# A decoder layer on one core: half a key projection set between two weighting steps, a norm's scalings moved behind the spikes, one division per group of heads

## The reference, cut to what matters

```
x = x + attn(layernorm(x), ...)                 # Mamba forward and backward, then FFN
x = x + xattn(layernorm(x), ctx, ctx, mask)     # 16 heads of 16
x = x + ffn(layernorm(x), W_fc, W_proj)

def xattn(query, key, value, mask):
    q, k, v = query @ wq.T + bq, key @ wk.T + bk, value @ wv.T + bv   # split into 16 heads
    scores = where(mask == 0, -1e9, einsum('bhqd,bhkd->bhqk', q, k) / sqrt(16))
    out = einsum('bhqk,bhkd->bhqd', softmax(scores), v)               # heads side by side again
    return out @ wo.T + bo

def ffn(x, W_fc, W_proj):
    y = square(relu(x @ W_fc.T)) @ W_proj.T
    for 5 steps: mem = 0.9 * mem + y - (mem > 1);  spikes += (mem > 1)
    return spikes / 5
```

## Time and profile before

| | us | share of the span |
|---|---|---|
| runs of the kernel, median of 3 | 2731.34 | |
| profiled execution | 2730.98 | |
| its span | 2729.2 | 100% |
| PE busy (matmuls) | 2585.1 | 95% |
| DVE busy | 2283.9 | 84% |
| ACT busy | 1743.3 | 64% |
| POOL busy | 1602.4 | 59% |
| mean granted PE clock | 0.984 | |

### The profile page before, as it was taken

How to read it: one execution, slowest core, us unless ns; L and a number is a source line. 1 busy time by engine, 2 the same in 40 slices (tenths; PEclk the granted TensorE clock), 3 DMA queues, 4 the chain that set the end, 5 groups by cost and what they waited for, 6 DMA issues and landing times. The chain is left out here.

```text
span 2729.2 us, 54786 instructions
## 1 busy us (share of the span) xinstructions
PE 2585.1 (95%) x18901; PEld 1767.7 (65%) x18934; DVE 2283.9 (84%) x3333; ACT 1743.3 (64%) x2871; POOL 1602.4 (59%) x886
## 2 busy tenths in 40 slices
PE   6999999999999999999998888999999999999995
PEld 3887787787777778777787764455454545454523
DVE  5999999999999899999999949686869595959684
ACT  4878877877977888788788633635354545444342
POOL 3999999999999999999999932111111111111010
PEclk9999999999999999999999999999999999999978
DMA  3122212212221221222122042404040404040300
GB/s 124 43 74 79 82 48 79 92 36 72 89 72 52 81 82 44 71 82 80 50 77 98 17 152 87 114 11 123 2 123 2 123 2 123 2 123 2 108 2 16
DMA packets 102089, 187.07 MB, mean 69 GB/s; under 512 B 14720, under 2 KB 75264, under 8 KB 100256
## 3 DMA queue, kind: packets, MB, share of 16 engines
q1 hardware_dynamic: 101840, 183.92, 21.4%
HBM read 148.38 MB, written 35.52 MB: 67 GB/s over the span
## 5 line engine op out<-in xcount | busy, mean ns | idle before, releaser
L983 DVE TENSOR_TENSOR_SCAN h<-dA,pair 128x512 f32<-128x512 f32 x1024 | 1172.6, 1201 | 101.9 <-PE pair L476 90.6
L1122 POOL TENSOR_TENSOR hC<-h,C_rep 128x1024 f32<-128x1024 f32 x512 | 1200.8, 2370 | 72.2 <-DVE h L983 64.5
L720 ACT ACTIVATE dA<-delta,cols 128x511 f32<-128x511 f32 x1024 | 664.2, 710 | 33.8 <-DVE h L983 27.7
L476 PE MATMUL pair<-diagB,duT 64*128 64x128 f32 x8192 | 549.3, 281 | 24.9 <-DVE h L983 15.6
L476 PEld LDWEIGHTS pair<-diagB,duT 64*128 64x128 f32 x8192 | 486.4, 188 | 126.8 <-issue 96.9
L577 PE MATMUL y_bank<-ident,hC 128*128 128x128 f32 x3980 | 521.6, 277 | 12.4 <-POOL hC L1122 10.5
L577 PEld LDWEIGHTS y_bank<-ident,hC 128*128 128x128 f32 x3980 | 440.3, 141 | 105.1 <-issue 50.5
L1912 DVE CUSTOM_DVE_ANT_0 masked<-pair,mask_bias 128x512 f32<-128x512 f32 x512 | 321.8, 687 | 19.9 <-PE pair L1380 13.6
L1999 POOL TENSOR_SCALAR rstd<-mv 128x4 f32<-128x4 f32 x24 | 23.8, 992 | 453.5 <-DVE mv L1743 451.6
L1633 ACT ACTIVATE pr<-pair 128x1024 f32<-128x1024 f32 x256 | 248.4, 1022 | 50.3 <-PE pair L1380 50.2
L2028 POOL CAST m_part<-m_rest 8x512 bf16<-8x512 f32 x16 | 9.7, 604 | 415.2 <-ACT m_rest L1633 415.2
(11 more groups left out here) (185 smaller groups left out, 3240.5 us busy)
## 6 DMA issues: line engine op xcount, KB each, us to landing
C_rep<-c_rows SPq DMA_DIRECT2D x128, 512.0 KB, 4.0
qk_parts<-qk_part SPq DMA_DIRECT2D x96, 256.0 KB, 4.1
w_in<-w_in SPq DMA_DIRECT2D x16, 1024.0 KB, 4.8
k_st<-qk_parts SPq DMA_DIRECT2D x8, 1536.0 KB, 9.1
q_st<-qk_parts SPq DMA_DIRECT2D x8, 1536.0 KB, 9.4
x_in<-x SPq DMA_DIRECT2D x18, 512.0 KB, 4.1
w_out<-w_out SPq DMA_DIRECT2D x17, 512.0 KB, 4.3
mid<-x_out SPq DMA_DIRECT2D x9, 512.0 KB, 4.8
```

Of the source, the lines that this page charges most:

```text
L476: return pe.matmul(o, lhsT, rhs, start=start, stop=stop)
L720: return act.activation(o, i, fn, **kw)
L983: last = dve.tensor_tensor_scan(h[:, g % 4, i, :], dA[:, g % 4, i, :], dBu[:, i, :], 0.0, ALU.mult, ALU.add)
L1122: last = pool.tensor_tensor(hC[:, g % RING], h[:, g % 4], C_rep[:, 2 * j:2 * j + 2, :], ALU.mult)
```

## The change

Three edits, in PE's and DVE's functions of the attention pass. On PE, `project_k` can be called for a part of its sum over the input features; the first half of the next element's first key projection now stands between `weigh(7, 0)` and `weigh(7, 1)`, and the second half where the whole stood. On DVE, the four divisions of a group become one operation over all four blocks of tokens. And DVE's order behind `keep_exp(7)` becomes `normalise(2)`, `finish`, `norm_apply`, `normalise(3)`, where it was `finish`, `normalise(2)`, `normalise(3)`, and the `norm_apply` behind `keep_exp(1)` goes.

```diff
--- before.py
+++ after.py
@@ -1451,9 +1451,17 @@
                                         ident[:, :])
                 last.then_inc(G.full_sem(("mt", i)), 1)
 
-            def project_k(beta, m, it):
-                pe.wait_ge(s_ctx.sem, s_ctx.count(beta))
-                project(("k", m), lambda k: w_att[:, 1, k, m * P:(m + 1) * P], lambda k: ctxT[:, k, :], KD, it)
+            def project_k(beta, m, it, parts=range(KD)):
+
+                key = ("k", m)
+                if 0 in parts:
+                    pe.wait_ge(s_ctx.sem, s_ctx.count(beta))
+                    pe.wait_ge(*G.free(key, it))
+                bk = G.bank(key, it)
+                for k in parts:
+                    last = mm(bk[:, :], w_att[:, 1, k, m * P:(m + 1) * P], ctxT[:, k, :], k == 0, k == KD - 1)
+                if KD - 1 in parts:
+                    last.then_inc(G.full_sem(key), 1)
 
             def project_v(jj, it):
                 project_tokens(("v", jj), tok(ctxT), lambda k: w_att[:, 2, k, :], KD, jj, it)
@@ -1587,11 +1595,13 @@
                     for half in range(2):
                         if unit + 1 < H // 2:
                             score(b, unit + 1, half)
+                        elif half == 1 and more:
+                            project_k(b + 1, 0, it, (0,))
                         weigh(b, unit, half, it)
                     if unit % 2 == 0 and unit > 0:
                         to_tokens(unit // 2 - 1, it)
                 if more:
-                    project_k(b + 1, 0, it)
+                    project_k(b + 1, 0, it, (1,))
                 to_tokens(H // 4 - 1, it)
                 if more:
                     project_k(b + 1, 1, it)
@@ -1803,10 +1813,8 @@
                 dve.reciprocal(rsum[:, :, :], o[:, :, :, DH:DH + 1].squeeze(3))
                 dve.drain()
                 dst = o_sb[:, :, g * 4 * DH:(g + 1) * 4 * DH].rearrange("p j (h e) -> p j h e", h=4)
-                for j in range(TT):
-                    last = dve.tensor_tensor(dst[:, j], o[:, j, :, 0:DH],
-                                             rsum[:, j, :].unsqueeze(2).broadcast_to((P, 4, DH)), ALU.mult)
-                last.then_inc(G.done_sem(("ot", g)), 1)
+                dve.tensor_tensor(dst, o[:, :, :, 0:DH], rsum[:, :, :].unsqueeze(3).broadcast_to((P, TT, 4, DH)),
+                                  ALU.mult).then_inc(G.done_sem(("ot", g)), 1)
 
             def spikes(beta, cols_of=(A3,)):
 
@@ -1920,8 +1928,6 @@
                 keep_exp(b, 0)
                 step(1, (1, 2))
                 keep_exp(b, 1)
-                if more:
-                    norm_apply(ATT, b + 1, x1n, xn_q)
                 step(2, (0,))
                 keep_exp(b, 2)
                 step(2, (1, 2))
@@ -1938,8 +1944,10 @@
                 keep_exp(b, 6)
                 step(4, (1, 2))
                 keep_exp(b, 7)
+                normalise(2, it)
                 finish()
-                normalise(2, it)
+                if more:
+                    norm_apply(ATT, b + 1, x1n, xn_q)
                 normalise(3, it)
                 if more:
                     cut_lo(b + 1, 0)
```

## The result

The changed kernel took 2741.31 us (median of 9 runs, 2737.18 to 2744.18) against 2731.52 us for the kernel before (median of 9, 2728.81 to 2733.31): a ratio of 1.0032, 95% interval 1.0023 to 1.0040. The forecast was 2737.5, the range ended at 2740. The direction was right, the time lies 1.3 us outside. The profiled execution took 2739.3 us, its span is 2737.5 us, 8.3 more than before. So of the 3.8 us between the forecast and the median, 2.1 are in the trace (8.3 where 6.2 was forecast), and the rest is that the median lies 2.0 us above the profiled execution, where 0.36 was assumed.

The account below looks back on a forecast made before the run. The output transfer's landing, then ACT's four copies, was taken to set the start of `wo`, with PE's list 0.17 us ahead. Seven rounds at +0.92 less 0.20 gave +6.2: 2731.34 + 6.2 = 2737.5 us, range 2732 to 2740.

Parts of the forecast that it names:

- What bounds the kernel, and the order of `finish`: Behind `keep_exp(7)`: later `finish` delays the output's landing, ACT's copies and `wo` by 0.92 us in each of seven rounds.
- The half projection: PE's gap ahead of `weigh(7, 1)` takes in 0.9 us of work, which comes out again as waiting for DVE and ACT.
- The single division: DVE's normalisation: one 128x256 operation at 417 ns for four in 0.62 us, saving 0.20 us a group.
- rival 3: DVE's division saves more, up to 0.40 us a group (0.47 by the skill's rule): +4.6, 2735.9 us; chance 0.06.
- The moved scalings: DVE's 1.38 us of norm scalings taken from behind `keep_exp(1)`: worth nothing there, ACT being only 0.04 us away.
- The last round: No next element and no wait for the output; PE waits 1.04 us for `normalise(3)`, so the shorter division gives 0.20 us.
- From there the order is as it was, everything hangs on `wo`: Behind the start of `wo`: nothing has slack to take in the delay, so all 0.92 us a round stays.
- The first round: Counted as one of the seven loop rounds, each 0.92 us longer.
- The sum: Whole profiled execution: 7 x 0.92 - 0.20 = +6.2 us, 2730.98 to 2737.2 us.
- The offset of the median, and the spread of the runs: Measured time against profile: median 0.36 us above the profiled execution, spread of runs 1 us.
- The upper bound of the sum: With the division losing 0.06 us a group, 1.18 us a round: 8.3 + 0.1 = +8.4 us.
- Rival 1: The output's landing does not hold ACT, `wo` follows PE: 0.7 us gained a round, 2726.2 us; chance 0.10.

Follow-up runs that it names:

- early_finish_whole: Changed kernel with spikes pulled ahead so `finish` stands before `keep_exp(7)`, key projection whole again behind `weigh(7, 1)`: 2732.75 us, ratio 1.0009, round 133.71 us.
- half_only: Kernel before, with only half of the next key projection moved between the last two weighting steps: 2730.98 us, ratio 0.9999, round 133.51 us.
- order_only: Kernel before, with only `normalise(2)` put ahead of `finish`: 2740.07 us, ratio 1.0031, round 134.62 us.
- finish_first: Changed kernel with `finish` back ahead of `normalise(2)`, directly behind `keep_exp(7)`: 2733.55 us, ratio 1.0012, round 133.70 us.
- one_division_only: Kernel before, with only the four divisions of a group made one of 128x256: 2732.16 us, ratio 1.0006, round 133.71 us.
- padded_once: Changed kernel with 12 idle semaphore increments of DVE ahead of its first round, run once: 2737.57 us, ratio 1.0024, round 134.43 us.
- own_tmp: Changed kernel with `tmp` in its own memory, so ACT doesn't wait for the output transfer: 2727.79 us, ratio 0.9987, round 133.10 us.
- once_16: Changed kernel with 16 idle semaphore increments of DVE ahead of its first round, run once: 2739.09 us (one execution), round 134.72 us.

## Why the prediction was right in its mechanism and wrong in its size

- **What bounds the kernel, and the order of `finish`:** right in the loop's rounds, to 0.01 us. The wait for the landing decides when `wo` starts; shift 0.92 forecast, 0.92 seen; issue 0.28 behind the end of `finish`, release 3.04 behind the issue, both as carried over. PE's path was not 0.17 us ahead of the landing's but level with it (`early_finish_whole`), which changes nothing in the sum.
- **The half projection:** right. It fills the gap and is worth 0.01 us alone (`half_only`).
- **The single division:** 425 ns against the 417 estimated, mean of the four of a round; saved 0.20 a group as taken, where rival 3 has 0.40 or 0.47. Rival 3 is out.
- **The moved scalings:** right, no effect on the units.
- **The last round:** right. PE's wait ahead of its transposes is 0.85 us (1.04).
- **"From there the order is as it was, everything hangs on `wo`":** this is the step that failed first. The order of the work was as it was, but not the place of the code. I priced the single division by its duration alone and left out that it also takes 12 instructions out of every round, and so moves the code of the maxima, where DVE and PE hand over to each other every 0.6 us. Measured price: 134.63 - 134.43 = 0.20 us a round, 1.2 us in the six distances, for an edit that the sum had as a gain.
- **The first round** is written out in DVE's list and not part of its loop, and I priced it as one of seven: the second term that failed. From the start of the pass (the clearing of `y_sb`) to ACT's first key copy it takes 92.67 us for 90.84, +1.83 in place of 0.92. Of that 0.63 is another gap in its maxima, which comes and goes: `order_only`, which has as many DVE instructions as the kernel before, has it as well, and `finish_first`, with as few as the changed one, doesn't. The remaining 0.28 is the gap ahead of `finish`, 0.45 us put down to issue, which delays the transfer. `one_division_only` has the same gap there and 0.34 beyond the landing's shift; `padded_once` has none there and -0.08. `finish_first` has 0.84: its gap lies behind `finish`, but the transfer took 3.81 us from issue to landing, where every other first round has 2.96 or less. A packet of the instruction queue ran among its packets; that it held the transfer up is not shown.
- **The sum** on the profiled execution, from these: 0.06 ahead of the pass + 1.83 + 6.71 in the six distances - 0.25 behind the last key copy = +8.35, as measured (8.3).
- **The offset of the median, and the spread of the runs,** failed as well. I took the changed kernel's median 0.36 us above its profiled execution, as before; it is 2.01 above. The spread I took as 1 us from three runs. Nine gave 4.5 us for the kernel before and 7.0 for the changed one. The medians differ by 9.8, the two profiled executions by 8.3; the interval of the ratio, 6 to 11 us, holds both. The upper bound of the sum, 2731.34 + 8.4 = 2739.7, left 0.3 us of the range for it. The trace's 2.1 us alone, or this offset alone, would have left the time inside the range; together they did not. Why the executions of the changed kernel spread more stays open.
- **Rival 1** (the landing does not hold ACT) is out by `half_only` and `own_tmp`.

## What to carry to other kernels

Before work is moved into a gap, find everything that ends at the next meeting point: here two paths ended together, and shortening one of them was worth nothing until the other was shortened too, when it was worth all of it. A store from a buffer that is used again can be part of the critical path, as here, so the operation that fills it comes before work that nobody waits for. And an instruction taken out of a list moves the code behind it: in a tight stretch of a loop expect some tenths of a microsecond a round either way, and compare rounds in the profile before blaming the edit.

## What the runs showed of the hardware

The cost of where code lies was not expected. With the same instructions in each loop round, and 0, 6, 12 or 16 idle ones ahead of the loop, the round took 134.63, 134.34, 134.43 and 134.72 us: 0.38 us between the best and the worst. A single gap in the loop's maxima is 0.41 to 0.43 us, put down to issue, and a packet of 8 KB on an instruction queue starts 0.6 us behind its end, in the changed kernel as in `once_16`. The packets' places move with the number of idle instructions of DVE.

The Trainium skill, "Runtime: NRT & Kernel Launch", section "Instruction fetch mechanics", says that an engine's sequencer fetches its program in blocks by a DMA queue of its own, and that crossing a block is mostly hidden. Here the row maxima show it hidden in some places and not in others. That the gap is such a fetch is not shown, only that it depends on the place.
